# Moving the convolution's history from VectorE to ScalarE in a state-space block on one Trainium2 core

## What is computed

```python
proj = x @ in_proj_w
hidden, gate = jnp.split(proj, 2, axis=-1)
h = jnp.swapaxes(hidden, 1, 2)
h = jax.lax.conv_general_dilated(h, conv_w, window_strides=(1,), padding=((KCONV - 1, KCONV - 1),),
                                 feature_group_count=INTER)[..., :L]
h = h + conv_b[None, :, None]
hs = jnp.swapaxes(jax.nn.silu(h), 1, 2)
ssm_p = hs @ x_proj_w
...
def step(s, inp):
    dA_t, dBu_t, C_t = inp
    s = dA_t * s + dBu_t
    y = jnp.einsum('bdn,bn->bd', s, C_t)
    return (s, y)
```

## Time and profile before

| | |
|---|---|
| median of 3 runs | 5266.09 us (5265.92 to 5266.54) |
| the profiled execution | 5265.83 us, of which the span of its instructions 5264.0 us |
| PE, DVE, ACT, POOL busy over the span | 92%, 84%, 51%, 61% |
| PE clock granted, mean | 0.973 |
| first scan / last scan | 92.4 us / 3668.5 us |
| from the first scan of a chunk to that of the next | 223.65 us in most, up to 224.45 us |
| busy in one chunk's length, 2000 to 2223 us | PE 210.81, DVE 198.85, POOL 157.37, ACT 139.62 us, PE clock 1.00 |

### The profile page before, as it was taken

One profiled execution on the slowest core, in us unless ns is written; L12 is line 12 of the kernel. 1 busy time (PEld: TensorE's weight loads), 2 busy tenths in 40 slices (PEclk: granted clock), 3 DMA queues, 4 the chain that ended last, 5 costly groups with the idle time before them and its releaser, 6 DMA issues. The chain is left out here.

```text
span 5264.0 us, 108717 instructions
## 1 busy us (share of the span) xinstructions
PE 4829.6 (92%) x44199; PEld 2786.0 (53%) x44199; DVE 4430.6 (84%) x7283; ACT 2702.7 (51%) x4373; POOL 3192.8 (61%) x1665
## 2 busy tenths in 40 slices
PE   7899999999999999999999999987799999999973
PEld 3444444444444444444444444433588888888862
DVE  4889889898898989889898898987488888888876
ACT  4656666656665666666566666554233333333330
POOL 2676776767767676676767767677234444344436
PEclk9999999999999999999999999998899999999985
DMA  2122222222122221222222222244300000000003
GB/s 103 77 103 75 100 87 89 101 77 105 65 105 95 83 105 73 97 91 87 103 75 101 85 89 101 77 156 181 127 28 26 26 28 26 26 28 26 26 31 70
DMA packets 120079, 415.65 MB, mean 79 GB/s; under 512 B 27040, under 2 KB 28704, under 8 KB 84128
## 3 DMA queue, kind: packets, MB, share of 16 engines
q1 hardware_dynamic: 110336, 397.01, 20.9%
q0 software_dynamic: 7776, 10.67, 0.9%
q10 hardware_dynamic: 1472, 1.04, 0.1%
HBM read 358.68 MB, written 49.99 MB: 78 GB/s over the span
## 5 line engine op out<-in xcount | busy, mean ns | idle before, releaser
L421 POOL TENSOR_TENSOR s<-s,Cb 128x1024 f32<-128x1024 f32 x1024 | 2395.6, 2361 | 968.5 <-DVE state L784 963.2
L779 DVE TENSOR_TENSOR_SCAN s<-s,state,BU 128x512 f32<-128x512 f32 x2048 | 2452.6, 1259 | 350.8 <-PE BU L870 337.0
L613 ACT ACTIVATE s<-dt,ch 128x512 f32<-128x512 f32 x2048 | 1306.9, 715 | 719.3 <-PE Y L887 718.0
L887 PE MATMUL Y<-s,ident 64*64 64x512 f32 x8192 | 1006.5, 607 | 68.6 <-POOL s L421 68.3
L813 PE MATMUL PJ<-xnT,w_in 128*128 128x512 f32 x2048 | 947.2, 606 | 29.6 <-ACT xnT L462 15.0
L870 PEld LDWEIGHTS BU<-spread,dtuT 32*128 32x128 f32 x16384 | 511.9, 188 | 521.1 <-DVE s L779 322.6
L870 PE MATMUL BU<-spread,dtuT 32*128 32x128 f32 x16384 | 609.4, 285 | 138.0 <-DVE s L779 134.9
L813 PEld LDWEIGHTS PJ<-xnT,w_in 128*128 128x128 f32 x2048 | 370.0, 190 | 502.5 <-issue 424.0
L887 PEld LDWEIGHTS Y<-s,ident 64*64 64x64 f32 x8192 | 276.3, 133 | 563.8 <-issue 535.2
L861 PE MATMUL PJ<-w_out,u 128*128 128x512 f32 x960 | 445.7, 607 | 6.9 <-ACT xnT L462 6.4
L658 DVE SCALAR_TENSOR_TENSOR u<-hid,ch,u 128x512 f32<-128x512 f32 x384 | 287.5, 749 | 19.8 <-issue 0.6
(11 more groups left out here) (242 smaller groups left out, 6933.2 us busy)
## 6 DMA issues: line engine op xcount, KB each, us to landing
Cb<-bc SPq DMA_DIRECT2D x256, 1024.0 KB, 4.8
x1t<-x SPq DMA_DIRECT2D x64, 256.0 KB, 2.6
out<-r_t SPq DMA_DIRECT2D x64, 256.0 KB, 2.1
xt<-in_x SPq DMA_DIRECT2D x31, 512.0 KB, 5.4
res<-in_x SPq DMA_DIRECT2D x62, 256.0 KB, 5.2
x<-res SPq DMA_DIRECT2D x62, 256.0 KB, 5.1
w_in<-in_factors SPq DMA_DIRECT2D x5, 1024.0 KB, 7.9
w_parts<-w_in SPq DMA_DIRECT2D x5, 1024.0 KB, 9.0
```

The costliest lines, as they stand in the source:

```text
L421: nc.gpsimd.tensor_tensor(pair, pair, Cb[q % 2][:, 2 * part * T:2 * part * T + 2 * T], ALU.mult).then_inc(z_ready, 1)
L613: nc.scalar.activation(s[k % SLOTS][:, n, :], dt[p % 2][:, gi, :], ACT.Exp, scale=ch[:, 2 * p + gi, 7 + 4 * nq + n:8 + 4 * nq + n]).then_i ...
L779: nc.vector.tensor_tensor_scan(s[k % SLOTS][:, n, :], s[k % SLOTS][:, n, :], BU[:, n::4], state[:, b, k, n:n + 1], ALU.mult, ALU.add).then ...
L887: last_ = nc.tensor.matmul(Y[r][y_rows(r, gi), :], ident[rows, rows], s[(k_even + gi) % SLOTS][rows, n, :], start=False, stop=(n == 3 and ...
```

## The change

The three-column copies leave VectorE. ScalarE fills the buffer's first columns from `hist` before it waits for the projection, drains, and, when the bank is full, takes the new history out of PSUM itself (the bank's last three columns) ahead of the two passes it already did. VectorE's `conv` now has a wait and three taps. `hist` is now read and written by ScalarE alone. The semaphore of POOL's first memsets gets a name of its own, since ScalarE waits for it too.

```diff
@@ in mamba_block
-        consts_ready = sem("consts_ready")
+        consts_ready, hist_cleared = sem("consts_ready"), sem("hist_cleared")
@@ GpSimd, at the start
             nc.gpsimd.memset(hist[:], 0.0)
-            pool.drain().then_inc(consts_ready, 1)
+            pool.drain().then_inc(hist_cleared, 1)
@@ ScalarE
             def take_hid(ring_, m, period, c_next, slot):
 
+                past = hist[:, c_next % BATCH, m, :]
                 wait(act, conv_done, c_next * G + m - 1)
+                nc.scalar.copy(hid[m % 2][:, 0:3], past)
+                act.drain()
 
                 act.wait_ge(ring_.full, ring_.filled(("hid", m), period))
                 bank = PJ[ring_.bank(("hid", m))]
+                nc.scalar.copy(past, bank[:, T - 3:T])
                 nc.scalar.activation(u[slot][:, m, :], bank[:], ACT.Identity, bias=ch[:, m, 4:5], scale=ch[:, m, 3:4])
                 nc.scalar.copy(hid[m % 2][:, 3:T + 3], bank[:]).then_inc(ring_.taken["act"], 1)
...
+            act.wait_ge(hist_cleared, 1)
             for m in range(G):
                 take_hid(ahead, m, 0, 0, 0)
@@ VectorE
-            def conv(ring_, m, period, b_next, slot):
+            def conv(ring_, m, period, slot):
 
                 out = u[slot][:, m, :]
                 h_ = hid[m % 2]
-                nc.vector.tensor_copy(h_[:, 0:3], hist[:, b_next, m, :])
-                s_, v = ring_.emptied(("hid", m), period)
-                dve.drain()
-                dve.wait_ge(s_, v)
-                nc.vector.tensor_copy(hist[:, b_next, m, :], h_[:, T:T + 3])
+                dve.wait_ge(*ring_.emptied(("hid", m), period))
                 for tap in range(3):
...
-            dve.wait_ge(consts_ready, 1)
+            dve.wait_ge(hist_cleared, 1)
             for m in range(G):
-                conv(ahead, m, 0, 0, 0)
+                conv(ahead, m, 0, 0)
...
-                            conv(steady, HID_AT[k - 1], c, 1 - b, 1 - b)
+                            conv(steady, HID_AT[k - 1], c, 1 - b)
@@ TensorE
-            pe.wait_ge(consts_ready, 2)
+            pe.wait_ge(consts_ready, 1)
```

## The result

| | before | changed |
|---|---|---|
| median | 5266.01 us (5263.25 to 5266.84, 6 runs) | 5244.89 us (5241.23 to 5248.58, 6 runs) |
| profiled execution, its span | 5265.83, 5264.0 us | 5245.41, 5243.6 us |
| first scan / last scan | 92.4 / 3668.5 us | 92.3 / 3643.6 us |
| most chunks | 223.65 us | 222.04 us |
| the 15 chunks that prepare another | 3356.7 us | 3331.4 us |

The ratio is 0.9961, with a 95% interval of 0.9949 to 0.9974: 0.4% faster, within 2 us of the forecast of 5243.4. The loop gained 24.7 us: 25.3 in the fifteen chunks with a convolution, against the 22.5 forecast, less 0.6 in the last chunk, which prepares nothing.

The account below looks back on a forecast made before the run. VectorE was taken to set the pace in most convolution steps, TensorE and ScalarE limiting the gain: 1.50 us a chunk in 15 chunks, 22.5 us, so 5265.83 - 22.5 + 0.1 = 5243.4 us; range 5230 to 5258.

Parts of the forecast that it names:

- VectorE's saving of 0.30 us a convolution: On VectorE, two copies, drain and wait go in each of 8 convolutions: 2.4 us a chunk added up without any limit.
- The extra 0.09 us of the first copy: First copy slowed by GpSimd's products, 0.23 instead of 0.14 us, in four steps; the first tap would meet the same delay.
- TensorE's limit in step 16: Step 16's input has no TensorE wait ahead of it, so its scans come 0.30 us earlier, not VectorE's 0.58.
- ScalarE late for the first tap of step 18: ScalarE empties group 4's bank late: this convolution gives 0.09 us, not 0.30; VectorE newly waits about 0.2 us.
- ScalarE's copies at 0.36 us a group: Cost added to ScalarE per take_hid: 0.27 us for the copy from `hist` with drain, 0.09 us for the PSUM copy.
- The idle time of 0.14 us: Ahead of ScalarE's pass over dt, before step 20's scans: TensorE still ends last, with 0.14 us in hand.
- TensorE's limit in step 20: Step 20's scans wait for TensorE and come 0.90 us earlier; the idle time ahead grows from 0.24 to about 0.6 us.
- step 21: Its scans come 1.20 us earlier, against 0.90 at step 20; the first tap was taken to meet the copy's 0.09 us.
- The rule of the Trainium skill: VectorE's first tap would stand for the full 0.20 us overlap with GpSimd, felt only in step 21: 1.7 us less gain.
- Given back behind step 24: Rival: TensorE's own list, not VectorE's scans, paces the chunk as a whole, so no gain: 5266 us; chance 0.08.
- Ahead of the loop: Where TensorE paces the convolutions, only the last take_hid's PSUM copy shows: +0.09 us, an estimate.

## Why the prediction was right, step by step

How much earlier each step's scans came than before, within a chunk (medians over the chunks), beside what the prediction said:

| step | 15 | 16 | 17 | 18 | 19 | 20 | 21 | 22 |
|---|---|---|---|---|---|---|---|---|
| predicted, us | 0.29 | 0.30 | 0.60 | 0.90 | 0.99 | 0.90 | 1.20 | 1.50 |
| measured, us | 0.31 | 0.31 | 0.63 | 0.95 | 1.09 | 0.95 | 1.26 | 1.63 |

- VectorE's saving of 0.30 us a convolution: measured 0.31 in step 14 (7.40 to 7.09 us from scans to scans), 0.33 in step 16, 0.31 in step 20. The extra 0.09 us of the first copy shows in three steps (15, 19 and 21), not in four as the prediction has it.
- TensorE's limit in step 16: right. The scans wait 0.29 us there, and the pair of runs with the transposes moved shows that it is TensorE's list and that it binds only with the change.
- ScalarE late for the first tap of step 18: right. 0.2 us were forecast, 0.17 measured, and the run without any history shows that the chunk doesn't pay for it.
- ScalarE's copies at 0.36 us a group: measured 0.31. The idle time of 0.14 us that was to be left ahead of the pass over dt is 0.23. The run with more copies confirms both the place and the price beyond.
- TensorE's limit in step 20: right, 0.74 us of waiting ahead of its scans against about 0.6.
- The term that was mis-sized is step 21: 0.30 us forecast, 0.37 measured (7.46 to 7.09 us). I had let the first tap inherit the 0.09 us that GpSimd's products cost the copy. By their rows, whose spans are rough on GpSimd, they run 0.2 us into the first tap too, but the three taps take 2.42 us in step 15 and 2.40 in step 21, beside 2.39 in step 14, where nothing of GpSimd's runs into them. With the small excesses of the other steps that makes 1.6 us a chunk for 1.50.
- The rule of the Trainium skill (SBUF — State Buffer, section on SBUF's two separate sides) would have had the tap, which reads two operands from SBUF, stand until GpSimd had finished. The rows show 0.01 to 0.03 us. Here the measurement decides.
- Given back behind step 24: fell. TensorE waits 0.61 us ahead of step 24's input as before, and a chunk keeps all of its gain.
- Ahead of the loop 0.09 us more were forecast. The first scan came 0.14 us earlier, and over the nine traces it scatters from 90.6 to 92.4 us, so this term can't be told.
- Not foreseen: what is lost outside the loop. The mechanism was right and a little too small (25.3 us in the fifteen chunks, not 22.5), and the median's 21.1 us came out so near the forecast's 22.4 because about 4 us went elsewhere. That part is luck. In the one execution where it was traced it was the longer wait for transfers behind the loop.

## What to carry to other kernels

When two engines pace a loop in turns, follow one period step by step and ask at each step which of the two ends last; here a saving of 0.29 to 0.38 us in each of 8 steps on VectorE, 2.65 us in all, was worth 1.6 us, and the two steps where TensorE took over could be named from its waits, or from their absence. Here the work moved to ScalarE was free as long as it fitted the idle time ahead of the one pass that others wait for (0.86 us), and cost nearly its full price beyond it, though the engine is busy for only half the time. Once the old bound is relieved, look at the neighbour's list again: an edit that had been worth nothing was worth 5 us. And when a stretch at half the clock grows, look at whether the engine worked or waited in it before the clock is blamed.

## What the runs showed of the hardware

- On ScalarE a three-column copy out of PSUM is 0.16 us long, but the pass behind it starts 0.06 us after it; one out of SBUF is 0.19 us long, and with a drain behind it the next copy starts 0.25 us after it.
- On VectorE a three-column copy that starts while GpSimd's tensor product still runs, by the rows, takes 0.23 us instead of 0.14. A multiply-add over 128x512 in the same place loses 0.01 to 0.03 us.
- The same 0.5 KB transfer (`tile_no`), issued at the same place, landed 25.2 us after its issue in one execution and 30.6 us in another.
- Most chunks of a kernel agree within 0.02 us between executions, while the whole time scatters: 5258.15 to 5270.13 us over 21 runs of the kernel before. A difference of a few microseconds can be read from the chunks where the medians can't tell it.
